# Softmax without a division of the probabilities: the sums' reciprocals are spread through DRAM and applied to the attended values

## The reference, cut to what matters

```python
xn, ln = _ln(x, g_x, b_x), _ln(latents, g_l, b_l)      # x: the context, latents: the sequence
q = ln @ w_q
k, v = split(concat([xn, ln], axis=1) @ w_kv)
sim = einsum('bhid,bhjd->bhij', q * scale, k)           # masked
attn = softmax(sim)
out = einsum('bhij,bhjd->bhid', attn, v)
return _ln(out @ w_out, g_o, b_o)
...
x = x + tanh(g_xattn[0]) * attention(ctx, layernorm(x), ...)
x = x + tanh(g_ffn[0]) * moe(layernorm(x), ...)         # top 2 of 8 experts with capacity
x = x + tanh(g_xattn[1]) * second_attention(layernorm(x), ctx, ctx, ...)
x = x + tanh(g_ffn[1]) * second_moe(layernorm(x), ...)
```

## Time and profile before

| what | us |
|---|---|
| median of 3 runs | 2225.14 (2224.73 to 2228.25) |
| profiled execution, span of the core | 2225.1 |
| one step in the middle of the first stage | 33.60 |
| PE busy, whole span | 2186.7 |
| DVE busy, whole span | 1728.1 |
| ACT busy, whole span | 1282.0 |
| POOL busy, whole span | 645.1 |

### The profile page before, as it was taken

One profiled execution on the slowest core, in us unless ns is written; L12 is line 12 of the kernel. 1 busy time (PEld: TensorE's weight loads), 2 busy tenths in 40 slices (PEclk: granted clock), 3 DMA queues, 4 the chain that ended last, 5 costly groups with the idle time before them and its releaser, 6 DMA issues. The chain is left out here.

```text
span 2225.1 us, 48355 instructions
## 1 busy us (share of the span) xinstructions
PE 2186.7 (98%) x15486; PEld 1865.5 (84%) x15486; DVE 1728.1 (78%) x6112; ACT 1282.0 (58%) x3251; POOL 645.1 (29%) x1162
## 2 busy tenths in 40 slices
PE   8999999999999999999999999999999999999997
PEld 6777777777777777777699999999878888888886
DVE  6788888888888888888675555555579999999986
ACT  6776776776776776776443333433345555555553
POOL 1123223222232232232220000000355555555541
PEclk9999999999999999999899999999999999999999
DMA  5320110110110110110052222221212222222210
GB/s 189 124 97 22 37 40 23 37 39 21 40 38 20 39 39 20 40 32 27 11 161 73 81 86 72 81 77 41 89 58 65 65 65 64 65 65 65 65 39 20
DMA packets 111642, 129.57 MB, mean 58 GB/s; under 512 B 14898, under 2 KB 98089, under 8 KB 111264
## 3 DMA queue, kind: packets, MB, share of 16 engines
q1 hardware_dynamic: 98249, 105.06, 14.9%
q0 software_dynamic: 12288, 21.21, 3.3%
q10 hardware_dynamic: 855, 0.19, 0.0%
HBM read 84.26 MB, written 54.53 MB: 62 GB/s over the span
## 5 line engine op out<-in xcount | busy, mean ns | idle before, releaser
L711 ACT ACTIVATE a_prob<-a_prob,a_nmax 128x376 f32<-128x376 f32 x512 | 309.7, 606 | 155.3 <-DVE a_nmax L857 155.3
L1457 ACT ACTIVATE e_hidden<-e_first,keep_b 128x256 f32<-128x256 f32 x320 | 134.1, 471 | 283.3 <-PE e_first L80 282.8
L857 DVE CUSTOM_DVE_ANT_0 a_prob<-a_score,a_mask_row 128x376 f32<-128x376 f32 x512 | 266.6, 540 | 10.8 <-issue 5.6
L80 PE MATMUL e_second<-e_w,e_hidden 128*128 128x256 f32 x1920 | 239.5, 284 | 0.0
L80 PEld LDWEIGHTS e_second<-e_w,e_hidden 128*128 128x128 f32 x1920 | 232.6, 192 | 0.0
L869 DVE TENSOR_SCALAR a_prob<-a_prob,a_rden 128x376 f32<-128x376 f32 x512 | 220.9, 453 | 2.5
L1151 PE MATMUL a_turned<-keep_ident,a_prob 128*128 128x128 f32 (+1 forms) x1536 | 217.3, 277 | 2.8 <-DVE a_probT L876 1.6
L1151 PEld LDWEIGHTS a_turned<-keep_ident,a_prob 128*128 128x128 f32 (+1 forms) x1536 | 173.5, 142 | 43.5 <-issue 27.6
L1142 PE MATMUL a_score<-a_kT,a_qT 64*128 64x376 f32 x1024 | 196.4, 502 | 0.0
L876 DVE COPY a_probT<-a_turned 128x384 f32<-128x384 f32 x256 | 139.8, 546 | 54.4 <-PE a_turned L1151 54.4
L719 ACT ACTIVATE a_probT<-a_turned 128x384 f32<-128x384 f32 x256 | 124.9, 488 | 92.1 <-PE a_turned L1151 91.7
(11 more groups left out here) (237 smaller groups left out, 5231.1 us busy)
## 6 DMA issues: line engine op xcount, KB each, us to landing
w_in<-W SPq DMA_DIRECT2D x32, 512.0 KB, 4.1
slots<-a_zeros SPq DMA_DIRECT2D x8, 1280.0 KB, 8.7
keep_rows<-slots SPq DMA_DIRECT2D x40, 256.0 KB, 3.9
answers<-e_y SPq DMA_DIRECT2D x40, 256.0 KB, 2.2
a_xn<-x SPq DMA_DIRECT2D x32, 256.0 KB, 2.9
a_xr<-x SPq DMA_DIRECT2D x32, 256.0 KB, 3.8
x<-r_x SPq DMA_DIRECT2D x32, 256.0 KB, 4.0
w_in<-x SPq DMA_DIRECT2D x32, 256.0 KB, 2.6
```

What stands on the lines that cost most here:

```text
L80: last = nc.tensor.matmul(out, stationary(a, t), moving(b, t), start=start and n == 0, stop=stop and n == len(todo) - 1)
L711: nc.scalar.activation(prob[:, u % 4, a], prob[:, u % 4, a], ACT.Exp, bias=nmax[:, u % 4, a:a + 1], scale=-1.0, accum_out=den[:, u % 4, a: ...
L857: nc.vector.tensor_tensor_reduce(prob[:, u % 4, a], score[SCORE_AT[u][a]][:, 0:NKV], mask_row[:, p], -1.0, 3.0e38, ALU.add, ALU.min, nmax[ ...
L1457: nc.scalar.activation(hidden[:, 2 * j + i], first[:, j, i * CH:(i + 1) * CH], ACT.Relu, bias=b1[:, 2 * j + i, bass.ds(e, 1)]).then_inc(re ...
```

## The change

The exponentials are turned as they are, without `normalise`. The sum's reciprocal is applied to the product with the values instead. There the queries lie along the row, so each of the 128 partitions (64 channels of each of two heads) needs the reciprocals of its head as a row of 256. To get them there, SP writes the pair's `rden` (128 partitions x 4) to a small DRAM tensor `shares` and reads it back with each head's row repeated over 64 partitions, into `share` (`spread_shares`, four times a batch; SP waits for the write to land before it issues the reads). `attended` on DVE multiplies product and shares into `att`, and so frees the PSUM bank: PE's waits for `att_lo` become waits for `att_ok`, but for that of `output`. `att_high` reads `att` and stands behind `turned_out` in ACT's order. `att_low` moves from DVE to GpSimd. `over_sum` is taken once for a pair (128x4) in place of once for a group (128x2). PE's order is unchanged. The diff shows, in this order, SP, GpSimd, ACT, DVE and PE; the further changes of DVE's step follow in words.

```diff
+            def spread_shares(b, m):
+                done = KI * b + m
+                eng.wait_ge(rden_ok, done + 1)
+                at_least(eng, share_in, 32 * (done - KI + 1))
+                eng.dma_start(t["shares"][m].rearrange("i a q -> q (i a)"),
+                              rden[:, m % 2].rearrange("p i a -> p (i a)"),
+                              allow_slow_non_contiguous=True).then_inc(share_out, 16)
+                eng.wait_ge(share_out, 16 * (done + 1))
+                at_least(eng, att_ok, done - KI + 1)
+                for a in range(2):
+                    eng.dma_start(share[64 * a:64 * a + 64, m].rearrange("p (i q) -> p i q", i=QT),
+                                  t["shares"][m, :, a].partition_broadcast(64)) \
+                        .then_inc(share_in, 16)
...
             def step(s, p):
                 if live(s - 1):
                     load_residual(s - 1, 1 - p)
                 if here(s - 4):
                     store(eng, s - 4, p)
+                if live(s - 2):
+                    spread_shares(s - 2, 1)
+                    spread_shares(s - 2, 2)
+                    spread_shares(s - 2, 3)
                 if live(s + 2):
                     load(s + 2, p)
+                if live(s - 1):
+                    spread_shares(s - 1, 0)
                 if isinstance(s, int) and s < N_CLEAR // 2:
                     clear_slots(2 * s)
                     clear_slots(2 * s + 1)
...
+            def att_low(b, m):
+                eng.wait_ge(att_hi, KI * b + m + 1)
+                nc.gpsimd.tensor_tensor(att2[:, 1, m], att[:, m], att2[:, 0, m].bitcast(F32),
+                                        ALU.subtract).then_inc(att_lo, 1)
             def step(s, p):
                 q = 1 - p
                 if isinstance(s, int) and s == 4:
                     eng.wait_ge(zeroed, 16 * N_CLEAR)
+                if live(s - 3):
+                    att_low(s - 3, 3)
                 if here(s - 3):
                     norm1(eng, s - 3)
                 if routed(s - 5):
                     dispatch(eng, s - 5, q, range(QT, QT * 2))
+                if live(s - 2):
+                    att_low(s - 2, 0)
                 if live(s):
                     norm0(s)
                 if here(s - 3):
                     norm2(eng, s - 3)
+                if live(s - 2):
+                    att_low(s - 2, 1)
                 if routed(s - 4):
                     dispatch(eng, s - 4, p, range(QT))
+                if live(s - 2):
+                    att_low(s - 2, 2)
                 if live(s - 2):
                     residual(s - 2, p)
...
             def att_high(b, m):
-                eng.wait_ge(pv_made, KI * b + m + 1)
+                eng.wait_ge(att_ok, KI * b + m + 1)
                 at_least(eng, out_ok, b)
-                nc.scalar.activation(att2[:, 0, m], (bank_a if m == 1 else bank_b)[:, 0:S], ACT.Copy).then_inc(att_hi, 1)
+                nc.scalar.activation(att2[:, 0, m], att[:, m], ACT.Copy).then_inc(att_hi, 1)
...
-            def normalise(b, u, a):
-                eng.wait_ge(rden_ok, NG * b + u + 1)
-                nc.vector.tensor_scalar(prob[:, u % 4, a], prob[:, u % 4, a], rden[:, u % 4, a:a + 1], None, ALU.mult) \
-                    .then_inc(norm_ok[a], 1)
+            def attended(b, m):
+                eng.wait_ge(pv_made, KI * b + m + 1)
+                eng.wait_ge(share_in, 32 * (KI * b + m + 1))
+                at_least(eng, att_lo, KI * (b - 1) + m + 1)
+                nc.vector.tensor_tensor(att[:, m], (bank_a if m == 1 else bank_b)[:, 0:S], share[:, m],
+                                        ALU.mult).then_inc(att_ok, 1)
...
             def turn_prob(b, u):
                 for a in range(2):
-                    eng.wait_ge(norm_ok[a], NG * b + u + 1)
+                    eng.wait_ge(exp_ok[a], NG * b + u + 1)
```

More of the change, by code:

```diff
@@ L434, in attend @@
         den = sb("a_den", [P, 4, 2])
-        rden = sb("a_rden", [P, 4, 2])
+        rden = sb("a_rden", [P, 2, 2, 2])
+        share = sb("a_share", [P, KI, S])
+        att = sb("a_att", [P, KI, S])
         prob = sb("a_prob", [P, 4, 2, NKV])
@@ L800, in step @@
                     turned_out(s - 2, 7, 0)
+                    att_high(s - 2, 2)
                 if live(s - 1):
@@ L928, in step @@
                     weights_lower(3, wo[:], stage_o)
-                if live(s - 2):
-                    normalise(s - 2, 2, 0)
                 if live(s - 3):
-                    att_low(s - 3, 3)
+                    attended(s - 3, 3)
                 if live(s - 2):
@@ L937, in step @@
                     choose(eng, s - 4, 0)
+                if here(s - 4):
+                    choose(eng, s - 4, 1)
                 if live(s - 2):
                     row_max(s - 2, p, 5, 1)
-                if here(s - 4):
-                    choose(eng, s - 4, 1)
                 if isinstance(s, int) and s == B + 2:
                     w1_lower(1)
-                if live(s - 2):
-                    normalise(s - 2, 2, 1)
                 if here(s - 4):
@@ L954, in step @@
                 if live(s - 2):
-                    normalise(s - 2, 3, 0)
+                    over_sum(s - 2, 1)
                 if here(s - 4):
                     choose(eng, s - 4, 4)
-                if live(s - 2):
-                    normalise(s - 2, 3, 1)
+                if live(s - 1) and not (isinstance(s, int) and s == 1):
+                    kvin_low(s - 1, q, 0)
                 if here(s - 4):
@@ L962, in step @@
                 if live(s - 1) and not (isinstance(s, int) and s == 1):
[L963 removed]
+                    kvin_low(s - 1, q, 1)
                 if here(s - 4):
                     choose(eng, s - 4, 6)
[L966 to L967 removed]
+                if live(s - 3):
+                    out_stat(s - 3)
                 if here(s - 4):
                     choose(eng, s - 4, 7)
[L970 to L971 removed]
                 if live(s - 2):
                     turned_out(s - 2, 2, 1)
+                if live(s - 3):
+                    out_centre(s - 3)
                 if routed(s - 4):
                     counts_in(eng, s - 4, bank_b)
[L976 to L977 removed]
                 if live(s - 2):
@@ L980, in step @@
                     row_max(s - 2, p, 6, 1)
-                    over_sum(s - 2, 4)
-                    normalise(s - 2, 4, 0)
-                    normalise(s - 2, 4, 1)
-                    att_low(s - 2, 0)
+                    over_sum(s - 2, 2)
+                    attended(s - 2, 0)
                     turned_out(s - 2, 3, 1)
@@ L989, in step @@
                     out_norm(eng, s - 3, q)
-                if live(s - 2):
-                    over_sum(s - 2, 5)
-                    normalise(s - 2, 5, 0)
                 if live(s):
@@ L998, in step @@
                     x1_stat(eng, s - 3, q)
-                if live(s - 2):
-                    normalise(s - 2, 5, 1)
-                    over_sum(s - 2, 6)
                 if routed(s - 4):
                     place(eng, s - 4, p, 0)
-                if live(s - 2):
-                    normalise(s - 2, 6, 0)
-                if routed(s - 4):
-                    place(eng, s - 4, p, 1)
                 if live(s - 1):
@@ L1010, in step @@
                 if routed(s - 4):
+                    place(eng, s - 4, p, 1)
                     place(eng, s - 4, p, 2)
@@ L1016, in step @@
                 if live(s - 2):
-                    normalise(s - 2, 6, 1)
+                    attended(s - 2, 1)
                 if routed(s - 4):
@@ L1020, in step @@
                 if live(s - 2):
-                    att_low(s - 2, 1)
                     turned_out(s - 2, 5, 1)
@@ L1035, in step @@
                     row_max(s - 1, q, 2, 1)
-                    over_sum(s - 1, 0)
                 if live(s - 2):
-                    att_low(s - 2, 2)
+                    attended(s - 2, 2)
                 if here(s - 3):
@@ L1044, in step @@
                     row_max(s - 1, q, 3, 0)
-                    normalise(s - 1, 0, 0)
-                    normalise(s - 1, 0, 1)
+                if live(s - 1):
                     row_max(s - 1, q, 3, 1)
@@ L2544, in build @@
         keep["w1_loaded"] = ctx.enter_context(nc.semaphore("w1_loaded"))
+        t["shares"] = nc.dram_tensor("shares", (KI, QT, 2, P), F32, kind="Internal").ap()
         routing(nc, t, keep, ctx)
```

63 lines of the change are left out of this document (23 added, 40 removed).

## The result

The changed kernel takes 2732.61 us (median of 4), the kernel before 2226.69 in the same series: a ratio of 1.2264 [1.2226, 1.2301], 506 us slower. Forecast were 2235 us and at most 2245. The direction was right, and the time was outside the range by far.

What follows compares the result with a forecast made beforehand. TensorE, busy 98% of the span, was taken as the bound. On 2225.1 us: prologue -0.7, zeroed-slots stall +7.6, lost clock +2.5, stage's end +0.8, together +10.2, so 2235; range 2224.5 to 2245.

Steps and rivals of the forecast that it cites:

- Third, the shares' trip through DRAM: SyncE's write and reads in a steady step: 7 us, 15 at the slow end; shares arrive before their values product.
- the sum's own upper bound: All upper bounds added one way, with 6.8 us for the shares' write landing: 2245.4 us.
- Rival D: Shares arrive after the product each step, `attended` blocks VectorE, TensorE waits for the bank: 2266 at 1 us a step; chance 0.06.
- the steady step costs 0: Middle steps of the first stage: the additions on TensorE's path cost 0, so steps stay at 33.6 us.
- the zeroed slots: Head of step 4: GpSimd's low part waits for late clears, `output(1)` 7.6 us late (3.7 to 13.5), plus 2.5 of clock.
- the covers in ScalarE's order and GpSimd's low part: Before `output` in steady steps: key copy done 0.2 us ahead, low part 0.7 us ahead, so cost 0.
- Rival A: `output` waits each step for the low part or key copy: 3 to 9 us more, 2238 to 2245; chance 0.14.
- 0 for the removed `normalise`: Steady steps: 6.9 us less VectorE work a step is hidden behind TensorE and worth 0.
- rival C: The 0.39 us at each a_turned truly waits for `normalise`: 12 us back, 2223 with the stall, 2213 without; chance 0.05.
- near 21 us busy: VectorE's expected busy time in a 33.6 us step after the change, down from 28.2.
- the prologue: Start of the first stage: a TensorE wait for `normalise` mostly goes, net -0.7 us, between -2.7 and +0.3.
- the stage's end: `output(31)` has no other work to hide its operands, slower low part on GpSimd: +0.8 us, between 0.3 and 1.5.

Runs made afterwards that it cites:

- e1: The kernel before with one more DMA write to DRAM in steps 5 to 32, in seven shapes, its landing waited for by SyncE alone: 2230.98 us.
- e3: The changed kernel with the shares written as 128 elements of 16 bytes, so in another order than the reads take: 2269.34 us, ratio 1.0198.
- e5: e3 with VectorE's last `choose` put ahead of `out_stat` again, as in the kernel before: 2254.0 us, ratio 1.012.
- e9: e8 with VectorE's `counts_in` put ahead of `out_centre` again, as in the kernel before: 2228.72 us, ratio 1.0013.
- e7: The kernel before with one exchange in VectorE's order, `out_stat` ahead of the step's last `choose`: 2257.12 us, ratio 1.0141.
- e10: The kernel before with one exchange in VectorE's order, `out_centre` ahead of `counts_in`: 2243.89 us, ratio 1.0079.
- e6: e5 with GpSimd's wait for the zeroed slots moved behind the low part of batch 1's last pair: 2244.94 us, ratio 1.0093.
- e13: The changed kernel unaltered, run again in a later series on one chip with e14: 2613.22 us, ratio 1.1752.
- e14: The changed kernel with both VectorE orders and the zeroed wait put right, the 4-byte write kept: 2614.09 us, ratio 1.1726.
- e8: The changed kernel with 16-byte write and matching reads, last `choose` ahead of `out_stat`, and zeroed wait behind the low part: 2245.35 us, ratio 1.009.

## Why the prediction was wrong, step by step

**Failed: "Third, the shares' trip through DRAM".** The write was taken at 3.0 us with 6.8 as the upper bound, from rows of DMAs none of which writes 4-byte neighbours. It took 9.1 us (SyncE's waits), 13.5 as a probe in the kernel before (e1), and 1.6 as 16-byte elements (e3). The bound was wrong as well as the value. The second half of the failure is arithmetic that the row would have allowed: the trips were set against each pair's own slack, and not added up on SyncE, which runs them one after another. Four trips at the assumed 3 us and the issues beside them need some 20 us of 33.6 (4 x 4.5 and 2 for the loads and the store); at 6.8 some 35, more than the step, so that the sum's own upper bound should have had a price in each step. Rival D named the place but was priced at 1 us a step and at VectorE; the queue on SyncE made it 15.8 (49.4 - 33.6), which in 32 steps is about the 506 us.
A rule of the Trainium skill was weighed there (DMA: Bandwidth & Descriptors, § Specifications: below 512 bytes the engine reads, modifies and writes) and led to 6.8 and 2239. Its warning was right for this write. As a rule on size alone it does not tell slow from quick here: 4-byte elements 32 bytes or more apart took 2.7 us or less.

**Failed: the steady step costs 0.** The working priced ScalarE's order and GpSimd's low part, and gave VectorE's order no price. Two exchanges in it, `out_stat` with the last `choose` and `out_centre` with `counts_in`, cost TensorE about 1 us a step, some 32 us, where the slow write doesn't hide them: e5 gave back 15 and e9 16.6. Alone in the kernel before they cost 30.6 and 16.7 (e7, e10), so they don't add up. The lines stood in the change, but not among the quoted orders.

**Right in the mechanism: the zeroed slots.** Forecast 7.6 us of stall and 2.5 of clock; e3 shows 7.54 of stall, and moving the wait is worth 9.1 (e6 against e5). That the stall fits so well is luck: e3's write is not the one of the sum, and `output` came at 106.70 where the sum had 108.4, but TensorE was also ready 1.65 us earlier than before (99.16 for 100.81). In the changed kernel itself this stall is hidden under the write's (e13 against e14: no difference).

**Right: the covers in ScalarE's order and GpSimd's low part.** e9 keeps both and runs at 33.6 us a step. The low part, taken at 0.75 us, has a mean of 744 ns:

```profile
L642 POOL TENSOR_TENSOR a_att<-a_att 128x256 fp32r<-128x256 f32 x128 | 95.2, 744 | 905.4 <-ACT a_att L761 880.1 <-DMA slots<-a_zeros 19.3 <-issue 5.9
```

Rival A did not happen in the steady steps. **Right: 0 for the removed `normalise`**, and rival C falls: the 0.39 us gap of the earlier trace rows stays in e9, now put down to ScalarE's exponentials:

```profile
PEld a_turned L1162 <- ACT a_prob L747: 6.9, 18, 0.4
```

The reason given against C was wrong all the same: "issue" can be a wait for another engine, as at L1189 in e8. **Missed without effect:** VectorE "near 21 us busy" a step; in e9 it is 24.4 (72.5 of 100 us).

**The ends, read in e9's trace.** In the prologue the wait of 1.20 us is gone, 1.49 has become 1.34, and `output` of batch 0 waits 0.50 anew: -0.85, where -0.7 was forecast. At the stage's end TensorE's gap before `output` grew from 1.09 to 2.82, by 1.73 where 0.8 was forecast. Of the 0.9 that the forecast lacked, 0.7 is the low part, which takes 1.46 us there and not the 0.74 of the others:

```profile
1106.48 1.21 DVE L938 TENSOR_TENSOR keep_w<-w_in,keep_w 128x1024 fp32r<-128x1024 f32 x1
...
1106.82 1.46 POOL L642 TENSOR_TENSOR a_att<-a_att 128x256 fp32r<-128x256 f32 x1 [2.52 <-ACT a_att L761]
...
1108.42 4.45 PE L80 MATMUL keep_bank<-a_wo,a_att 128*128 128x256 f32 x24 [2.82 <-DVE r_pr L277]
```

VectorE's instruction, with two inputs in SBUF, had begun 0.34 us before. So GpSimd was held behind VectorE, which the prediction weighed for rival A and set aside "by the row". It is the only one of the 128 low parts that took longer than 0.85 us, in e3 and in the changed kernel too; nearly all others begin beside a `row_max`, which reads its scores from PSUM, and aren't held. Some of the gap came back, as `output` itself took 4.45 us in place of 5.31.

## What to carry to other kernels

When a change puts a wait for a DMA's landing into a queue, multiply it by the trips in a step and compare the sum with the step, before asking how much slack each trip has. A transposing write of 4-byte elements is priced by how many of them lie close together, not by its bytes; keep each partition's elements together and do the transposing in the reader's access pattern. In a hand-written order every exchanged pair of lines counts: ask for each which of the two waits for the bound engine, and which the bound engine waits for.

## What the runs showed of the hardware that was not expected

The packets of the shares' write had been moved in 1.2 us, and yet it counted as landed 9.6 us after its issue (median, as e1's expectation says from the trace). In the probes 2 KB as 512 neighbours of 4 bytes held SyncE for 13.5 us behind the issue, at distances of 8, 16 and 32 bytes 8.1, 4.3 and 2.7, at 512 bytes 2.2. Size made little difference at a distance of 16 bytes (4.3 for 4 bytes, 3.9 for 16). That writes to one short stretch of memory are done one after another fits this, but only the dependence on the distance is shown. The same kernel took 2733 us in one series and 2613 in another, while the kernel before differed by less than 0.1%: the landing of these writes depends on something that other DMAs here don't show. What that is, the chip or the moment, stays open, and so does why the landing is 9 us in the kernel and 13.5 in the probe, whose rows lay 64 KB apart.
